# Multiply-adds with a factor of 1.0 read from a column in SBUF, and fewer pieces a map, in a deformable-convolution kernel

## The chip, the cores and the metric

The kernel runs on one core of a Trainium2 chip. The metric is the device time of one execution in microseconds; of several executions the median counts. Engines are called TensorE (PE in the rows; PEld is its weight load), VectorE (DVE), ScalarE (ACT), GpSimd (POOL) and SyncE (SP).

## The reference

Input x is 4 images of 128 channels and 80 x 80 pixels in float32. What is computed, cut to what matters:

```
out_normal = conv3x3(x, w_normal)
offset     = conv3x3(x, [w_offx, w_offy])            # 18 channels: dy, dx of 9 taps
out_x      = deform_conv(x, offset, w_dx)            # bilinear samples at 9 shifted taps
out_y      = deform_conv(x, offset, w_dy)
out        = conv3x3(concat(out_normal, out_x, out_y), w_fusion)     # 384 -> 128 channels
out        = relu(bn1(out))
out        = bn2(conv3x3(out, w_conv2))
return relu(out + x)
```

`deform_conv` takes, for each pixel and tap, the four corners around a shifted position, weighs them bilinearly and multiplies the sample by the tap's 128 x 128 weights.

## The kernel before, in words

The work is cut into 40 strips of 8 rows (640 pixels, 5 tiles of 128 pixels; 10 strips an image), and a loop of 44 steps (`run_steps`) is written out for each engine. Step i deals with the samples of strip i, and in the same step with later stages of earlier strips: the sums for the fusion convolution of strip i-1, that convolution for strip i-2, the last convolution for strip i-4. A step has nine parts, one for each tap k. `SLICES` says which pieces of the convolutions ("O" offsets, "F" fusion, "N" normal, "C" last) TensorE does within each tap. The order of each engine's instructions is the order of this code; between engines there are only semaphores.

**Samples.** GpSimd issues an indirect DMA for each tile and tap (L350, 45 a strip, 1800 in all): for 128 pixels it fetches the cell with the corners, by indices in SBUF that VectorE computed (`indices`, L717 to L743). `cells` has 15 slots (`GSLOTS`), and a gather waits until the slot's earlier user has been read (`mixed_done`, L348) and until TensorE is within 25 tiles (`pace`, L349). For the first image the table is x itself and ScalarE makes the upper product (L567); for the other images the table holds slopes, which VectorE makes from x (`slopes`, L892, two pieces in each of the first 27 steps). VectorE mixes the two rows of corners (L756: five multiply-adds of 256 elements a tap, whose factor is a column of `wgt` in SBUF), ScalarE makes the left product (L575, in the rows under the helper's L535), and VectorE adds the right one (L762: five of 128 elements). TensorE turns the sample (L431), ScalarE copies it out as a high part (`samp_hi`, L534), VectorE subtracts that for the low part (`samples_low`, L708), and TensorE multiplies high and low parts (`three`, L386: L388, L391, L394).

**High and low parts.** Each convolution runs in float32r as three products of high and low parts. The high part is a ScalarE copy (L534); the low part is VectorE's `low` (L706 to L708): source minus high part, a tensor-tensor subtraction.

**The fusion convolution.** It works on pairs of rows of three maps `raw` (the three concatenated inputs), on four kinds of rows held in `d_raw`/`d_hi`/`d_lo`, 16 rows of 82 each: rows 0 to 7 hold differences of rows two apart (`zs`, `last_row`), rows 8 to 11 sums, rows 12 to 15 differences of pairs (`sums`). VectorE makes them with `combine` (L830 to L832), a scalar-tensor-tensor instruction, a x 1.0 + b or - b, whose factor 1.0 is a constant within the instruction. In the rows `d_raw` is called `d_lo_f`.

VectorE's program in a step (L896 to L966), per tap k: `last_row` (k = 1), `sample` for tap k + 2, `samples_low` for k + 1, `indices` at k = 3, `last_row_low` at k = 2, a piece of `slopes` at k = 2 and 6, then what follows on a finished piece of a convolution:
- k = 4 (F, 1): L925, L927 (both read PSUM), `sums`: 6 combines of 320 elements
- k = 5 (F, 2): L934, `sums_low`: 6 subtractions of 320 elements
- k = 6 (F, 3): L941, `zs`: 6 combines of 240 elements and one for the first row; then L950, two multiply-adds of 320 elements with constant 0.0, which make the low part of the intermediate map `mid`
- k = 7 (N, 0): `zs_low`: 3 subtractions of 320 and 3 of 240 elements
- k = 8 (N, 1): `x_low`, one subtraction of 820 elements

ScalarE waits for `sums_done` and `zs_done` before its one copy for each (`sums_high` L610, `zs_high` L615), and before it overwrites `raw` (L678, L679). The first four steps use `FIRST_SLICES`.

Of the kernel before, what the change touches and what calls it, by code (L numbers as in the profile page):

```python
# [7 lines left out]
F32 = mybir.dt.float32  # L8
F32R = mybir.dt.float32r
I32 = mybir.dt.int32  # L10
ALU = mybir.AluOpType
# [3 lines left out]
B, C, H, W = 4, 128, 80, 80  # L15
TAPS = 9
EPS = 1e-5
ROWS = 8
# [83 lines left out]

BN_STEPS = 10
NIDX = 10
NCONST = 128 + 2 * TILES * TAPS + 4 * (STEPS + 1)


class Flags:
# [30 lines left out]
def at_least(eng, sem, value):  # L139

    if isinstance(value, int) and value <= 0:
        return
    eng.wait_ge(sem, value)


def deform_block(nc, x, xflat, xpair, weights, bn, const, out):
    ctx = ExitStack()
    with ctx:
# [24 lines left out]
        base_y = cst[:, 128:128 + PER].rearrange("p (j k) -> p j k", k=TAPS)  # L173
        base_x = cst[:, 128 + PER:128 + 2 * PER].rearrange("p (j k) -> p j k", k=TAPS)
        per_strip = 128 + 2 * PER

        x_raw = sb("x_raw", [128, SLOT])
        x_hi = sb("x_hi", [128, 2, SLOT_ROWS, PITCH], F32R)
# [352 lines left out]
        def _(eng):  # L531
# [82 lines left out]

            def zs_high(s):  # L615

                at_least(eng, zs_done, 7 * s + 7)
                copy(d_hi[:, :, 0:Z_ROWS - 1, 1:1 + W], d_raw[:, :, 0:Z_ROWS - 1, 1:1 + W]).then_inc(zs_hi, 1)
                at_least(eng, last_done, s)
                copy(keep[:], raw[:, :, ROWS - 2:ROWS, :]).then_inc(keep_done, 1)  # L620

            def step(i, par, fl):
                for k in range(TAPS):
# [21 lines left out]
                    for job, q in fl.done[k]:  # L645
# [30 lines left out]
                        if job == "N" and fl.strip:  # L676
                            rows = slice(q * HR, q * HR + HR)
                            at_least(eng, sums_done, 6 * i)  # L678
                            at_least(eng, zs_done, 7 * i)  # L679
                            at_least(eng, keep_done, i)  # L680
                            at_least(eng, n_done, 2 * i + q + 1)
                            copy(raw[:, 0, rows, :], work[q][:, 0:HALF].rearrange("p (r w) -> p r w", w=W))\
                                .then_inc(n_out, 1)
                            if q == 1 and fl.load:
                                x_high(i + 2, par)
# [19 lines left out]
        def _(eng):  # L705
# [123 lines left out]

            def combine(dst, a, b, op):  # L830

                return eng.scalar_tensor_tensor(out=dst, in0=a, scalar=1.0, in1=b, op0=ALU.mult, op1=op)  # L832

            def sums(s):

# [8 lines left out]
            def zs(s):  # L844

                for g in range(3):
                    to = d_raw[:, g, :, 1:1 + W]
                    combine(to[:, 1:HR, :], raw[:, g, 0:HR - 1, :], raw[:, g, 2:HR + 1, :], ALU.subtract).then_inc(zs_done, 1)
                    combine(to[:, HR:Z_ROWS - 1, :], raw[:, g, HR - 1:ROWS - 2, :], raw[:, g, HR + 1:ROWS, :],
                            ALU.subtract).then_inc(zs_done, 1)  # L850
                to = d_raw[:, :, :, 1:1 + W]
                if s % STRIPS:
                    at_least(eng, keep_done, s)
                    ins = combine(to[:, :, 0, :], keep[:, :, 1, :], raw[:, :, 1, :], ALU.subtract)
                else:
                    ins = eng.tensor_scalar(to[:, :, 0, :], raw[:, :, 1, :], -1.0, None, ALU.mult)
                ins.then_inc(zs_done, 1)

            def sums_low(s):

                at_least(eng, sums_hi, s + 1)
                for g in range(3):
                    for first in (SUM_ROW, DIFF_ROW):
                        rows = slice(first, first + PAIRS)
                        ins = low(d_lo[:, g, rows, 1:1 + W], d_raw[:, g, rows, 1:1 + W], d_hi[:, g, rows, 1:1 + W])
                ins.then_inc(sums_low_done, 1)

            def zs_low(s):

                at_least(eng, zs_hi, s + 1)  # L870
                for g in range(3):
                    for rows in (slice(0, HR), slice(HR, Z_ROWS - 1)):
                        ins = low(d_lo[:, g, rows, 1:1 + W], d_raw[:, g, rows, 1:1 + W], d_hi[:, g, rows, 1:1 + W])
                ins.then_inc(zs_low_done, 1)

            def last_row(s):
# [19 lines left out]
            def step(i, par, fl):  # L896
                for k in range(TAPS):
# [21 lines left out]
                    for job, q in fl.done[k]:  # L919
# [18 lines left out]
                        if job == "F" and q == T - 1:  # L938
# [5 lines left out]
                                zs(i - 1)  # L944
                            if fl.fuse:
                                at_least(eng, mid_hi_done, s + 1)
                                for half in range(2):
                                    rows = slice(half * HR, half * HR + HR)
                                    to = slice(1 + half * HR, 1 + half * HR + HR)
                                    ins = eng.scalar_tensor_tensor(  # L950
                                        out=mid[:, par, 1, to, 1:1 + W], in0=mid_f[:, rows, :], scalar=0.0,
                                        in1=mid[:, par, 0, to, 1:1 + W].bitcast(F32),
                                        op0=ALU.max, op1=ALU.subtract)
                                ins.then_inc(mid_lo_done, 1)
                        if job == "N" and q == 0 and fl.rows:
                            zs_low(i - 1)
# [14 lines left out]
def shape_constants():  # L971
# [8 lines left out]
    for s in range(STEPS + 1):  # L980
        b, r = s // STRIPS, s % STRIPS
        c[:, 128 + 2 * PER + 4 * s:128 + 2 * PER + 4 * s + 4] = (
            ROWS * r, max(b - 1, 0) * CELLS + LEAD * PITCH + 2, float(r != 0), float(r != STRIPS - 1))
    return c


# [40 lines left out]
```

## Time and profile before

| | us |
|---|---|
| median of 3 runs | 2667.61 |
| lowest, highest | 2664.85, 2673.97 |
| profiled execution | 2661.92 |
| its span | 2660.1 |

The profiled execution's mean granted TensorE clock is 0.966 of full speed. Busy shares of the span: TensorE 89% (15680 matmuls), VectorE 85% (5999 instructions), ScalarE 59%, GpSimd 75%. Busy time counts each engine's own instructions; semaphore waits and the issue of DMAs by SyncE are not in it. A share is an average over all stages, and an engine with a high share need not be the one that sets the time: for that one has to look at what ends each engine's idle time. Line numbers are those of the kernel before; a helper's line (L534, L535, L708, L832) stands for all who call it. Instructions of VectorE are recorded with overlap: the next one starts some 80 ns before the recorded end of the one ahead, so start-to-start times are shorter than the recorded durations.

### The profile page before, as it was taken

Reading aid. Unit: us, or ns where it says so; the run is one execution under the profiler, and the core shown is the slowest. Engines: PE = TensorE matmul, PEld = TensorE weight load, DVE = VectorE, ACT = ScalarE, POOL = GpSimd, SP = SyncE. Lnnn points to the kernel's source line nnn. Section 1 sums busy time; section 2 is a strip of 40 time slices with the busy share of each in tenths; the row PEclk is TensorE's granted clock in tenths of the full one; section 3 lists DMA queues with packets and bytes.
Section 4 is the critical chain, followed back from the end, with each engine's and each line's share of the span. In section 5 each row is a group of like instructions: output and inputs, shape, how many; then the busy total and the mean of one; then the engine's idle time right before and its main releaser. Section 6 shows DMA issues by size and latency. Waiting matters only on the chain.

```text
span 2660.1 us, 46973 instructions
## 1 busy us (share of the span) xinstructions
PE 2361.2 (89%) x15680; PEld 2323.2 (87%) x15680; DVE 2252.6 (85%) x5999; ACT 1565.6 (59%) x3577; POOL 2000.7 (75%) x1807
## 2 busy tenths in 40 slices
PE   3667899998999989989999999999989999899897
PEld 3567888998999989989899998998989988888897
DVE  5788888888998988988888898998888888888862
ACT  5777877877655555655555555555555555555531
POOL 7777777777777777777777777777777777777740
PEclk9879999999999999999999999999999999999999
DMA  7766777777777777777777777766666666666640
GB/s 223 214 213 211 241 229 222 227 226 222 220 226 241 220 227 232 228 233 233 233 231 240 239 238 225 234 206 206 200 205 195 207 197 204 198 196 206 194 126 25
DMA packets 179139, 564.89 MB, mean 212 GB/s; under 512 B 32721, under 2 KB 34129, under 8 KB 178769
## 3 DMA queue, kind: packets, MB, share of 16 engines
q0 software_dynamic: 144000, 471.97, 58.8%
q1 hardware_dynamic: 34896, 89.91, 9.6%
q8 instruction: 125, 2.05, 0.3%
q14 instruction: 118, 0.96, 0.1%
HBM read 527.41 MB, written 34.34 MB: 211 GB/s over the span
## 4 chain that ended last, share of the span: by engine, by line
DVE 38%; PE 26%; ACT 12%; DMA 11%; issue 9%; POOL 4%; ACTq 0%; DVEq 0%; POOLq 0%; SPq 0%
DVE mixed L756 9%; DMA cells<-slope_table,index 9%; DVE d_lo_f L832 6%; PE work L388 6%; PE work L391 5%; DVE d_lo L708 5%; PE work L394 5%; DVE samp L762 5%; DVE samp_lo L708 5%; ACT samp L535 4%; POOL cells L350 4%; ACT samp_hi L534 3%; DMA cells<-in_xpair,index 3%; PE turned L431 2%; PE acc L388 2%
## 5 line engine op out<-in xcount | busy, mean ns | idle before, releaser
L350 POOL DMA_INDIRECT cells<-slope_table,index x1350 | 1489.7, 1103 | 411.7 <-issue 208.8
L535 ACT ACTIVATE samp<-mixed,wgt 128x128 f32<-128x128 f32 x1800 | 649.1, 397 | 602.8 <-DVE mixed L756 600.0
L756 DVE SCALAR_TENSOR_TENSOR mixed<-cells,wgt 128x256 f32<-128x256 f32 x1350 | 575.6, 476 | 158.4 <-DMA cells<-slope_table,index 155.8
L350 POOL DMA_INDIRECT cells<-in_xpair,index x450 | 501.3, 1114 | 148.9 <-issue 86.3
L388 PE MATMUL work<-d_hi,w_hi 128*128 128x320 f32 x1440 | 480.9, 334 | 75.4 <-ACT off_s L534 73.6
L762 DVE SCALAR_TENSOR_TENSOR samp<-mixed,wgt,samp 128x128 f32<-128x128 f32 x1800 | 515.3, 345 | 29.8 <-ACT samp L535 29.3
L391 PE MATMUL work<-d_lo,w_hi 128*128 128x320 f32 x1440 | 464.4, 322 | 0.0
L394 PE MATMUL work<-d_hi,w_lo 128*128 128x320 f32 x1440 | 463.7, 322 | 0.0
L388 PE MATMUL acc<-samp_hi,w_hi 128*128 128x320 f32 x1440 | 451.3, 313 | 0.0
L391 PE MATMUL acc<-samp_lo,w_hi 128*128 128x320 f32 x1440 | 448.3, 311 | 0.0
L394 PE MATMUL acc<-samp_hi,w_lo 128*128 128x320 f32 x1440 | 447.3, 311 | 0.0
L431 PE MATMUL turned<-cst,samp 128*128 128x128 f32 x1800 | 264.5, 279 | 192.3 <-DVE samp_lo L708 173.9
L431 PEld LDWEIGHTS turned<-cst,samp 128*128 128x128 f32 x1800 | 213.6, 142 | 219.1 <-DVE samp L762 110.0
L388 PEld LDWEIGHTS work<-d_hi,w_hi 128*128 128x128 f32 x1440 | 282.3, 196 | 84.5 <-ACT off_s L534 82.2
L708 DVE TENSOR_TENSOR samp_lo<-turned,samp_hi 128x640 fp32r<-128x640 f32 x360 | 294.2, 817 | 47.7 <-ACT samp_hi L534 47.6
L391 PEld LDWEIGHTS work<-d_lo,w_hi 128*128 128x128 f32 x1440 | 283.7, 197 | 0.0
L394 PEld LDWEIGHTS work<-d_hi,w_lo 128*128 128x128 f32 x1440 | 283.2, 197 | 0.0
L534 ACT ACTIVATE d_hi<-d_lo_f 128x1920 fp32r<-128x1920 f32 (+2 forms) x120 | 153.2, 1277 | 213.0 <-DVE d_lo_f L832 207.2
L388 PEld LDWEIGHTS acc<-samp_hi,w_hi 128*128 128x128 f32 x1440 | 276.8, 192 | 0.0
L391 PEld LDWEIGHTS acc<-samp_lo,w_hi 128*128 128x128 f32 x1440 | 276.0, 192 | 0.0
L394 PEld LDWEIGHTS acc<-samp_hi,w_lo 128*128 128x128 f32 x1440 | 274.6, 191 | 0.0
L534 ACT ACTIVATE samp_hi<-turned 128x640 fp32r<-128x640 f32 x360 | 248.3, 690 | 20.5 <-PE turned L431 18.9
(86 smaller groups left out, 4198.5 us busy)
## 6 DMA issues: line engine op xcount, KB each, us to landing
cells<-slope_table,index POOLq DMA_INDIRECT x1350, 3.9
slope<-in_xpair SPq DMA_DIRECT2D x54, 384.0 KB, 5.3
slope_table<-slope SPq DMA_DIRECT2D x54, 384.0 KB, 4.1
x_raw<-in_xflat SPq DMA_DIRECT2D x40, 410.0 KB, 4.6
resid<-in_x SPq DMA_DIRECT2D x40, 320.0 KB, 5.2
out<-resid SPq DMA_DIRECT2D x40, 320.0 KB, 4.1
cells<-in_xpair,index POOLq DMA_INDIRECT x450, 3.9
w_lo_f<-in_weights SPq DMA_DIRECT2D x4, 576.0 KB, 8.6
```

Of the source, the lines that this page charges most:

```text
L350: eng.indirect_dma_start(out=cells[:, g, :], out_offset=None, in_=cell_rows, in_offset=bass.IndirectOffsetOnAxis(ap=index[:, par, j, k:k + ...
L388: ins = eng.matmul(dst, w_hi[:, w], hi, start=start, stop=False, skip_group_check=True)
L391: ins = eng.matmul(dst, w_hi[:, w], lo, start=False, stop=False, skip_group_check=True)
L394: return eng.matmul(dst, w_lo[:, w], hi, start=False, stop=stop, skip_group_check=True)
L431: ins = eng.transpose(turned[:, j * 128:(j + 1) * 128], samp[:, tp, j, :], ident)
L534: return eng.activation(dst, src, ACT.Copy)
L535: return eng.activation(dst, src, ACT.Copy, scale=scale)
L708: return eng.tensor_tensor(dst, src, hi.bitcast(F32), ALU.subtract)
L756: eng.scalar_tensor_tensor(out=both, in0=corner[:, g, :, 1, :], scalar=wgt[:, par, 1, 0, j, k:k + 1], in1=base, op0=ALU.mult, op1=ALU.add, ...
L762: eng.scalar_tensor_tensor(out=samp[:, tp, j], in0=mixed[:, tp, j, C:2 * C], scalar=wgt[:, par, 1, 1, j, k:k + 1], in1=samp[:, tp, j], op0 ...
L832: return eng.scalar_tensor_tensor(out=dst, in0=a, scalar=1.0, in1=b, op0=ALU.mult, op1=op)
```

## The change

The constant table gets two more columns, one of 0.0 and one of 1.0 (`zero`, `one`). `combine` takes its factor 1.0 from the column instead of from the instruction, for all its callers (sums, differences, last row, slopes). The low parts of the sums and of the differences are made by `combine` instead of the tensor-tensor subtraction, one instruction a map instead of two (640 and 560 elements). The differences are one instruction a map instead of two (480 elements), and the semaphore counts follow (4 a strip instead of 7). L950 becomes one instruction of 640 elements with its factor 0.0 from the column. The low parts of samples, x and weights, and `last_row_low`, stay as they are.

```diff
-NCONST = 128 + 2 * TILES * TAPS + 4 * (STEPS + 1)
+NCONST = 128 + 2 * TILES * TAPS + 4 * (STEPS + 1) + 2
...
+        zero, one = (cst[:, NCONST - n:NCONST - n + 1] for n in (2, 1))
...
-                at_least(eng, zs_done, 7 * s + 7)
+                at_least(eng, zs_done, 4 * s + 4)
...
-                            at_least(eng, zs_done, 7 * i)
+                            at_least(eng, zs_done, 4 * i)
...
-                return eng.scalar_tensor_tensor(out=dst, in0=a, scalar=1.0, in1=b, op0=ALU.mult, op1=op)
+                return eng.scalar_tensor_tensor(out=dst, in0=a, scalar=one, in1=b, op0=ALU.mult, op1=op)
...
-                    combine(to[:, 1:HR, :], raw[:, g, 0:HR - 1, :], raw[:, g, 2:HR + 1, :], ALU.subtract).then_inc(zs_done, 1)
-                    combine(to[:, HR:Z_ROWS - 1, :], raw[:, g, HR - 1:ROWS - 2, :], raw[:, g, HR + 1:ROWS, :],
-                            ALU.subtract).then_inc(zs_done, 1)
+                    combine(to[:, 1:Z_ROWS - 1, :], raw[:, g, 0:ROWS - 2, :], raw[:, g, 2:ROWS, :], ALU.subtract)\
+                        .then_inc(zs_done, 1)
...
-                    for first in (SUM_ROW, DIFF_ROW):
-                        rows = slice(first, first + PAIRS)
-                        ins = low(d_lo[:, g, rows, 1:1 + W], d_raw[:, g, rows, 1:1 + W], d_hi[:, g, rows, 1:1 + W])
+                    rows = slice(SUM_ROW, D_ROWS)
+                    ins = combine(d_lo[:, g, rows, 1:1 + W], d_raw[:, g, rows, 1:1 + W],
+                                  d_hi[:, g, rows, 1:1 + W].bitcast(F32), ALU.subtract)
...
-                    for rows in (slice(0, HR), slice(HR, Z_ROWS - 1)):
-                        ins = low(d_lo[:, g, rows, 1:1 + W], d_raw[:, g, rows, 1:1 + W], d_hi[:, g, rows, 1:1 + W])
+                    rows = slice(0, Z_ROWS - 1)
+                    ins = combine(d_lo[:, g, rows, 1:1 + W], d_raw[:, g, rows, 1:1 + W],
+                                  d_hi[:, g, rows, 1:1 + W].bitcast(F32), ALU.subtract)
...
-                                for half in range(2):
-                                    rows = slice(half * HR, half * HR + HR)
-                                    to = slice(1 + half * HR, 1 + half * HR + HR)
-                                    ins = eng.scalar_tensor_tensor(
-                                        out=mid[:, par, 1, to, 1:1 + W], in0=mid_f[:, rows, :], scalar=0.0,
-                                        in1=mid[:, par, 0, to, 1:1 + W].bitcast(F32),
-                                        op0=ALU.max, op1=ALU.subtract)
+                                ins = eng.scalar_tensor_tensor(
+                                    out=mid[:, par, 1, 1:1 + ROWS, 1:1 + W], in0=mid_f[:], scalar=zero,
+                                    in1=mid[:, par, 0, 1:1 + ROWS, 1:1 + W].bitcast(F32),
+                                    op0=ALU.max, op1=ALU.subtract)
...
+    c[:, NCONST - 1] = 1.0
```

## Rows read from the trace of the kernel before

**Rows 1.** The page: busy time by engine, and the chain of waits by engine.
```profile
PE 2361.2 (89%) x15680; PEld 2323.2 (87%) x15680; DVE 2252.6 (85%) x5999; ACT 1565.6 (59%) x3577; POOL 2000.7 (75%) x1807
...
DVE 38%; PE 26%; ACT 12%; DMA 11%; issue 9%; POOL 4%; ACTq 0%; DVEq 0%; POOLq 0%; SPq 0%
```

**Rows 2.** Groups of GpSimd (busy, mean ns, idle before), then durations min/median/max in ns.
```profile
L350 POOL DMA_INDIRECT cells<-slope_table,index x1350 | 1489.7, 1103 | 411.7 <-issue 208.8 <-DVE mixed L756 83.2 <-PE work L388 74.0
L350 POOL DMA_INDIRECT cells<-in_xpair,index x450 | 501.3, 1114 | 148.9 <-issue 86.3 <-DVE mixed L756 29.3 <-PE acc L388 12.4
...
L350 POOL DMA_INDIRECT cells<-slope_table,index x1350: 942/948/3922, 660.8 to 2560.6; - x193
L350 POOL DMA_INDIRECT cells<-in_xpair,index x450: 942/947/4781, 18.4 to 659.4; - x150
```

**Rows 3.** Timeline of GpSimd: start us, duration us, instruction, idle before and releaser.
```profile
18.44 3.27 POOL L350 DMA_INDIRECT cells<-in_xpair,index  x1 [8.24 <-DVE index L742]
...
1291.30 1.08 POOL L350 DMA_INDIRECT cells<-slope_table,index  x1 [0.31 <-issue]
...
1306.10 3.15 POOL L350 DMA_INDIRECT cells<-slope_table,index  x1 [0.30 <-issue]
1309.55 1.66 POOL L350 DMA_INDIRECT cells<-slope_table,index  x1 [0.30 <-PE work L388]
...
1350.36 3.29 POOL L350 DMA_INDIRECT cells<-slope_table,index  x1 [0.30 <-PE work L388]
...
1358.43 1.23 POOL L350 DMA_INDIRECT cells<-slope_table,index  x1 [0.30 <-issue]
...
2553.86 2.29 POOL L350 DMA_INDIRECT cells<-slope_table,index  x1 [0.30 <-issue]
...
2560.63 1.13 POOL L350 DMA_INDIRECT cells<-slope_table,index  x1 [0.30 <-issue]
```

**Rows 4.** Busy time by engine, from the last gather's end to the span's end.
```profile
2561.80:2660.10 98.30, 84.21 (x540) 83.23 (x538) 32.64 (x80) 22.22 (x40) 0.00 (x0) 0.97 0.08 28
```

**Rows 5.** Stretches of the transposes: strips 4 to 38, strip 17, strip 18 (second figure: length).
```profile
297.50:2512.30 2214.80, 226.31 (x1576) 183.72 (x1577) 257.33 (x315) 217.45 (x315) 0.98 0.71 220
...
1120.70:1187.30 66.60, 6.42 (x46) 5.28 (x46) 7.35 (x9) 6.22 (x9) 0.95 0.76 234
1187.30:1247.40 60.10, 6.41 (x45) 5.25 (x46) 7.35 (x9) 6.20 (x9) 1.00 0.72 224
```

**Rows 6.** VectorE's longest waits in strip 17, then in strip 18 (us, times, longest).
```profile
DVE mixed L756 <- DMA cells<-slope_table,index: 7.9, 8, 2.5
...
DVE samp_lo L708 <- ACT samp_hi L534: 1.6, 4, 0.8
```

**Rows 7.** Timeline of VectorE: start us, duration us of the group, instructions.
```profile
1290.28 2.49 DVE L832 SCALAR_TENSOR_TENSOR d_lo_f<-raw 128x320 f32<-128x320 f32 x6
...
1305.31 1.99 DVE L832 SCALAR_TENSOR_TENSOR d_lo_f<-raw 128x240 f32<-128x240 f32 x6
1307.21 0.40 DVE L832 SCALAR_TENSOR_TENSOR d_lo_f<-keep,raw 128x240 f32<-128x240 f32 x1
1307.53 0.88 DVE L950 SCALAR_TENSOR_TENSOR mid<-mid_f,mid 128x320 fp32r<-128x320 f32 x2
1308.34 2.06 DVE L756 SCALAR_TENSOR_TENSOR mixed<-cells,wgt 128x256 f32<-128x256 f32 x5
...
1350.34 2.49 DVE L832 SCALAR_TENSOR_TENSOR d_lo_f<-raw 128x320 f32<-128x320 f32 x6
1352.75 2.06 DVE L756 SCALAR_TENSOR_TENSOR mixed<-cells,wgt 128x256 f32<-128x256 f32 x5
...
1357.97 2.53 DVE L708 TENSOR_TENSOR d_lo<-d_lo_f,d_hi 128x320 fp32r<-128x320 f32 x6
1360.41 2.05 DVE L756 SCALAR_TENSOR_TENSOR mixed<-cells,wgt 128x256 f32<-128x256 f32 x5
```

**Rows 8.** VectorE's groups by shape: busy us, mean ns of one, idle before.
```profile
L727 DVE SCALAR_TENSOR_TENSOR pos<-off_s,cst 128x45 f32<-128x45 f32 x40 | 10.7, 268 | 1.4
...
L739 DVE SCALAR_TENSOR_TENSOR above<-cell_f 128x45 f32<-128x45 f32 x40 | 8.5, 212 | 0.0
```

## The prediction, before the kernel was changed

> **What bounds the kernel now.** I read the page first. TensorE is busy 89%, VectorE 85%, GpSimd 75%, and the chain of waits gives VectorE 38% and GpSimd only 4% [rows 1]. Read alone, that says "VectorE, then TensorE", and GpSimd looks free for a quarter of the time. The groups of GpSimd correct this. It issues 1800 gathers of mean 1.103 us (1.114 in the first image), with 411.7 + 148.9 us "idle" before them, mostly put down to "issue" [rows 2]. That idle time is no wait: in the timeline it is 0.30 us before every gather, whichever engine is named as releaser [rows 3]. So 1800 x 0.30 = 540 us of it is the gathers' own issuing, and little is left. Busy plus issuing is 1991 + 540 = 2531 us, and the time from the first gather (18.4) to the end of the last (2561.8) is 2543 us [rows 2, 3]. **GpSimd never stops**; it sets the time, with some 98 us behind its last gather in which the last strips are finished [rows 4].
>
> Are the others free? A strip (nine taps, 45 gathers) takes 2214.8 / 35 = 63.3 us over strips 4 to 38. But strip 18 took 60.1 us and strip 17 took 66.6 us [rows 5]. In strip 17 VectorE waited 7.9 us for gathered cells; in strip 18 its longest wait is 1.6 us in total, for ScalarE, and cells are not among its waits [rows 6]. So 60.1 us is what TensorE, VectorE and ScalarE need when the cells are there, and the rest is the gathers' pace.
>
> Why does a gather take 1.103 us, where the shortest is 942 ns and the median 948 [rows 2]? There are long ones: 76 of over 1.9 us (mean 3.01; the first, of 18.44, and the last, of 2553.86, stand in [rows 3]), and 55 of the gathers right behind them also take 1.72 us on average; the other 1669 take 1.00. I laid GpSimd's timeline over VectorE's [rows 3, 7]. The gather of 1306.10 (3.15 us) begins within L832's run of differences (from 1305.31), and ends 0.90 us behind the start of the first L756 (1308.34), that is, one undisturbed gather behind it. The gather of 1350.36 (3.29 us) begins as L832's sums begin (1350.34) and ends 0.90 us behind L756 at 1352.75. The same holds through L950, which follows the differences. So a gather that begins within a back-to-back run of multiply-adds with **constant** factor and both inputs in SBUF stands until the run is over. Of the 76 long ones 58 begin within L832. Not each run closes: the gather of 1291.30, within the sums from 1290.28, took only 1.08 us. Two other kinds do not hold it that way, though both their inputs lie in SBUF too: the subtractions L708 (the gather of 1358.43, within the run from 1357.97 to 1360.41, took 1.23 us, a wait of 0.28 to the end of the piece of 0.41), and L756, whose factor is a **column**, behind whose start the long ones end.
>
> **The change part by part.** VectorE first. Start to start, L832 of 320 elements takes 2.41 / 6 = 0.402 us and of 240 takes 1.90 / 6 = 0.317 [rows 7], so 1.05 ns an element and 0.066 us fixed. A factor from a column costs more: 45 elements take 268 ns with one (L727), 212 without (L739) [rows 8], so +0.056 us. A strip then gets:
> - sums: 6 x 0.402 = 2.41 becomes 6 x 0.458 = 2.75: +0.34
> - differences (480 elements, 3 for 6) and their first row: 2.22 becomes 3 x 0.626 + 0.37 = 2.25: +0.03
> - L950, 640 elements in one piece: 0.81 becomes 0.79: -0.02
> - low parts of the sums: 2.44 becomes 3 x 0.79 = 2.38: -0.06
> - low parts of the differences (560): 3 x 0.402 + 3 x 0.317 = 2.16 becomes 3 x 0.71 = 2.13: -0.03
> - last row +0.06; slopes +0.06 for each of 54.
>
> That is +0.26 us a strip in the taps where TensorE waits for VectorE, and 0.06 for the last row, which lies in a tap where VectorE waits for cells. If that cover goes, it costs 40 x 0.06 = 2 us. In total VectorE gets 40 x 0.32 + 3 = 16 us more. The constants' load grows by two columns: nothing, within a load already made. The waits on the count 4 s + 4 replace those on 7 s + 7; ScalarE waits for the whole set before and after, so nothing is late by it.
>
> GpSimd: what goes. A closed run costs, by the gather of 1306.10 and the one behind it, (3.15 - 0.95) + (1.66 - 0.95) = 2.91 us [rows 3]. 58 of them are 169 us. What comes: a gather within a column-factor piece waits for that piece's end. The bounds are nothing and a whole piece (0.46 to 0.79 us); I take a third of the piece, since the subtraction row shows 0.28 in a piece of 0.41 and most gathers (median 948) show none. About 4.6 gathers a strip begin in the sums, differences, last row and L950 (6 us of them, a gather each 1.3 us), at a third of a mean piece of 0.54, 0.18; 3.5 in the low parts at a third of 0.75, 0.25, of which 0.45 us is there today. Together 0.83 + 0.87 - 0.45 = 1.25 us a strip, 50 us. Net 169 - 50 = 119 us, 3.0 us a strip: GpSimd's own pace becomes 63.3 - 3.0 = 60.3 us.
>
> The rest of the kernel needs 60.1 + 0.26 + 0.06 (slopes) = 60.4. So **the gain is cut off by the next bound**, VectorE and TensorE in turn. Two bounds this close don't give the larger one exactly, since what one lacks in a strip is not made up in the next; I add 0.6 us (between 0 and the 3 us by which strips differ today): 61.0. Then 35 strips x (63.3 - 61.0) = 80 us. From the first four strips and the end I take nothing. The profiled execution took 2661.9 us (span 2660.1), so 2582; the median of the runs is 5.7 us above it, hence **2587 us**, 3% faster.
>
> One rule speaks against this. What the rows show is that the kind of factor decides how long a gather stands [rows 3, 7]. The Trainium skill ("SBUF — State Buffer", Who interferes with whom) says only that a VectorE instruction with two SBUF inputs contends with a GpSimd instruction that reads SBUF, and that the lock is held for the whole instruction. By that rule the kind of factor changes nothing and pieces of double length lock for longer; the time would be that of the first rival below, not 2587 us.
>
> **Rivals.**
> - *Locks go by instruction, not by run*. GpSimd could always slip in between two instructions and what matters is their length. Then the sums stay as they are, and longer pieces and VectorE's 0.32 us a strip come on top: 1.25 us of new waits a strip, without the 2.91s going: 35 x 1.25 = +44 on the median, **2712**. It decides if a column-factor run of sums, with its 0.46 us pieces, closes as before. Against it: gathers end behind the first L756, not behind one piece of L832. For it: L756 runs in fives, so a run of six or seven such instructions was never seen. Chance 0.07.
> - *VectorE sets the end as the chain says* (38%) and GpSimd's pace follows it: +16 us, **2684**. Against it: no gather waited over its 0.30. Chance 0.03.
> - *The gap opened by the column is sometimes missed* (some sums runs close today, some do not; L756 has stretched gathers too): half of the 2.91s remain, so GpSimd gains 85 - 50 = 35 us: **2633**. Chance 0.15.
> - *The first bound is further off*: strips 4 to 38 fall to 60.2 and the first four gain too: 35 x 3.1 = 109, **2559**. Chance 0.05.
> - *No change that can be seen*: relief and longer locks cancel. Chance 0.04.
>
> The forecast itself has the remaining 0.66.
>
> **Numbers.** The range reaches from 2553 (the waits of new pieces at their lower bound, the next bound at 60.2, and some us of the first strips) to 2640 (half the runs still close); 0.14 of the chance lies above it. A measurement of this kernel tells 0.3%, some 8 us, from no change: faster 0.86, same 0.04, slower 0.10.
>
> **What would show it.** Right: GpSimd's gathers of over 1.9 us nearly gone, and their mean 1.103 - 119 / 1800 = 1.04 us; VectorE (L756) waits less for cells; the spans of strips near 61 us and more even; L832 at 0.54 us for 320 elements (L832 as it is, plus 0.056), low parts of 640 elements in three pieces; ScalarE's offsets no longer hold up TensorE. Then GpSimd would show waits above 0.30 us, since it is no longer the one that never stops. Wrong: 3 us gathers within L832 as before (the first rival, or the third if half), or gathers that are short while the strips stay at 63 us, which would mean that 60.1 us is no floor that can be kept from strip to strip.

## The result, and the profile after

| | before | after |
|---|---|---|
| median, us | 2667.22 (4 runs) | 2797.19 (4 runs) |
| lowest, highest | 2664.85, 2673.97 | 2786.12, 2805.11 |
| profiled execution, its span | 2661.92, 2660.1 | 2786.12, 2784.3 |

The ratio is 1.048, with a 95% interval of 1.0439 to 1.0521: **slower by 130 us**, where 80 us less were forecast and 2640 was the end of the range. (Lines below are one higher than before: L350 is now L351, L756 is L757, L832 is L833; L950 is L948.)

The page of the changed kernel, beside [rows 1]:

```profile
PE 2395.6 (86%) x15680; PEld 2347.6 (84%) x15680; DVE 2271.9 (82%) x5599; ACT 1565.4 (56%) x3577; POOL 2124.3 (76%) x1807
...
PE 30%; DVE 26%; DMA 18%; issue 10%; ACT 10%; POOL 6%; ACTq 0%; POOLq 0%; DVEq 0%; SPq 0%
...
L757 DVE SCALAR_TENSOR_TENSOR mixed<-cells,wgt 128x256 f32<-128x256 f32 x1350 | 582.8, 479 | 252.9 <-DMA cells<-slope_table,index 249.2
```

VectorE has 19 us more work, but the span grew by 124. Of the chain, gathers and their transfers now hold 24% where they held 15%, and VectorE waits 249 us for cells. The engine to look at is again GpSimd. Its groups (as in [rows 2]), then its durations (min/median/max in ns):

```profile
L351 POOL DMA_INDIRECT cells<-slope_table,index x1350 | 1583.0, 1173 | 411.3 <-issue 254.7 <-DVE mixed L757 81.4 <-PE acc L389 45.4
L351 POOL DMA_INDIRECT cells<-in_xpair,index x450 | 531.6, 1181 | 148.3 <-issue 88.7 <-DVE mixed L757 28.6 <-PE acc L389 13.8
...
L351 POOL DMA_INDIRECT cells<-slope_table,index x1350: 942/949/5202, 690.3 to 2683.2; - x193
L351 POOL DMA_INDIRECT cells<-in_xpair,index x450: 942/947/5566, 17.6 to 689.1; - x150
```

The idle time is what it was, 0.31 us a gather, and the median gather too. What grew is the long ones. I call **standing time** what the gathers take beyond an undisturbed 0.946 us each: 1583.0 + 531.6 - 1800 x 0.946 = 412 us, where before it was 1991.0 - 1702.8 = 288 us. The difference, 124 us, is that of the spans. 118 gathers take over 1.9 us (76 before).

Busy time in stretches of the transposes: strips 4 to 38 (second figure: length), and all instructions from the last gather's end to the end of the span, beside [rows 4, 5]:

```profile
302.00:2636.60 2334.60, 232.61 (x1575) 185.19 (x1576) 257.71 (x315) 217.29 (x315) 0.96 0.69 209
...
2684.40:2784.30 99.90, 84.64 (x529) 83.44 (x527) 32.63 (x60) 22.21 (x40) 0.01 (x1) 0.92 0.08 28
```

A strip takes 2334.6 / 35 = 66.7 us instead of 63.3; the tail hardly changed (99.9 us for 98.3). So the loss lies in every strip, in the gathers. Their timeline (start us, duration us, idle before):

```profile
1161.66 1.21 POOL L351 DMA_INDIRECT cells<-slope_table,index  x1 [0.30 <-PE acc L389]
1163.17 1.29 POOL L351 DMA_INDIRECT cells<-slope_table,index  x1 [0.30 <-issue]
1164.76 2.99 POOL L351 DMA_INDIRECT cells<-slope_table,index  x1 [0.30 <-DVE mixed L757]
1168.05 0.96 POOL L351 DMA_INDIRECT cells<-slope_table,index  x1 [0.30 <-issue]
1169.32 5.20 POOL L351 DMA_INDIRECT cells<-slope_table,index  x1 [0.30 <-issue]
1174.82 0.94 POOL L351 DMA_INDIRECT cells<-slope_table,index  x1 [0.30 <-issue]
```

and VectorE's, in the same stretch (start, duration of the group):

```profile
1161.17 2.47 DVE L833 SCALAR_TENSOR_TENSOR d_lo<-d_lo_f,cst,d_hi 128x640 fp32r<-128x640 f32 x3
1163.55 2.06 DVE L757 SCALAR_TENSOR_TENSOR mixed<-cells,wgt 128x256 f32<-128x256 f32 x5
1165.53 1.40 DVE L763 SCALAR_TENSOR_TENSOR samp<-mixed,wgt,samp 128x128 f32<-128x128 f32 x5
1166.84 0.82 DVE L709 TENSOR_TENSOR samp_lo<-turned,samp_hi 128x640 fp32r<-128x640 f32 x1
...
1168.57 1.98 DVE L833 SCALAR_TENSOR_TENSOR d_lo_f<-raw,cst 128x480 f32<-128x480 f32 x3
1170.45 0.47 DVE L833 SCALAR_TENSOR_TENSOR d_lo_f<-keep,cst,raw 128x240 f32<-128x240 f32 x1
1170.83 0.89 DVE L948 SCALAR_TENSOR_TENSOR mid<-mid_f,cst,mid 128x640 fp32r<-128x640 f32 x1
1171.63 2.07 DVE L757 SCALAR_TENSOR_TENSOR mixed<-cells,wgt 128x256 f32<-128x256 f32 x5
1173.71 1.52 DVE L763 SCALAR_TENSOR_TENSOR samp<-mixed,wgt,samp 128x128 f32<-128x128 f32 x5
```

Take 0.95 us from the end of a gather: that is when it was let in. The gather of 1169.32 begins in the second of the differences, which now read their factor from a column as all behind them do, and is let in at 1173.57, as the last L757 ends and L763 starts 0.1 us late: the run was **not** opened by the column, and it no longer ends where L757 begins. The gather stood through eight boundaries. The gathers of 1161.66 and 1163.17 begin within low parts and are let in at 1161.92 and 1163.51, each as a piece ends. But then the next one, of 1164.76, begins 1.25 us on, just as the fourth L757 starts (1163.55 + 3 x 0.40), and stands until L709, which reads PSUM, at 1166.8.

Counted over the trace: of the long gathers before, 55 began in sums or differences and were let in at the first L756 behind them, with 2.20 us of standing each. In the changed kernel 29 that begin there stand until L763 starts, 3.74 us each; 74 begin in L757 and L763 (13 before).

### The profile page after: what moved, and what is told of

It reads as the page before. It is cut to its first block, busy times and chain, and to the rows that moved or that the text cites. A ratio compares the mean times of both kernels' runs of the same rounds, so it can differ in the third digit from the quotient of the medians.

```text
span 2784.3 us, 46573 instructions
## 1 busy us (share of the span) xinstructions
PE 2395.6 (86%) x15680; PEld 2347.6 (84%) x15680; DVE 2271.9 (82%) x5599; ACT 1565.4 (56%) x3577; POOL 2124.3 (76%) x1807
## 4 chain that ended last, share of the span: by engine, by line
PE 30%; DVE 26%; DMA 18%; issue 10%; ACT 10%; POOL 6%; ACTq 0%; POOLq 0%; DVEq 0%; SPq 0%
DMA cells<-slope_table,index 13%; PE work L389 7%; PE work L392 6%; PE work L395 6%; DVE mixed L757 6%; POOL cells L351 6%; DVE d_lo_f L833 5%; DMA cells<-in_xpair,index 4%; ACT samp L536 4%; DVE samp L763 4%; DVE samp_lo L709 4%; DVE d_lo L833 3%; PE turned L432 3%; ACT samp_hi L535 3%; PE acc L389 2%
## 5 line engine op out<-in xcount | busy, mean ns | idle before, releaser
L351 POOL DMA_INDIRECT cells<-slope_table,index x1350 | 1583.0, 1173 | 411.3 <-issue 254.7
L757 DVE SCALAR_TENSOR_TENSOR mixed<-cells,wgt 128x256 f32<-128x256 f32 x1350 | 582.8, 479 | 252.9 <-DMA cells<-slope_table,index 249.2
L351 POOL DMA_INDIRECT cells<-in_xpair,index x450 | 531.6, 1181 | 148.3 <-issue 88.7
L763 DVE SCALAR_TENSOR_TENSOR samp<-mixed,wgt,samp 128x128 f32<-128x128 f32 x1800 | 514.8, 347 | 33.1 <-ACT samp L536 32.5
L432 PE MATMUL turned<-cst,samp 128*128 128x128 f32 x1800 | 271.5, 284 | 268.9 <-DVE samp_lo L709 238.2
L709 DVE TENSOR_TENSOR samp_lo<-turned,samp_hi 128x640 fp32r<-128x640 f32 x360 | 294.6, 818 | 40.0 <-ACT samp_hi L535 39.8
```

What stands on the lines that cost most here:

```text
L351: eng.indirect_dma_start(out=cells[:, g, :], out_offset=None, in_=cell_rows, in_offset=bass.IndirectOffsetOnAxis(ap=index[:, par, j, k:k + ...
L432: ins = eng.transpose(turned[:, j * 128:(j + 1) * 128], samp[:, tp, j, :], ident)
L709: return eng.tensor_tensor(dst, src, hi.bitcast(F32), ALU.subtract)
L757: eng.scalar_tensor_tensor(out=both, in0=corner[:, g, :, 1, :], scalar=wgt[:, par, 1, 0, j, k:k + 1], in1=base, op0=ALU.mult, op1=ALU.add, ...
L763: eng.scalar_tensor_tensor(out=samp[:, tp, j], in0=mixed[:, tp, j, C:2 * C], scalar=wgt[:, par, 1, 1, j, k:k + 1], in1=samp[:, tp, j], op0 ...
```

## The experiments

Each was timed against the kernel before on the same chip. Its median there was 2664.64 us for e1 to e4, 2675.49 for e5 and e8 to e10, 2668.80 for e7 and e11 to e13, and 2674.43 for e14 and e15. So a difference of medians between two of these groups, or against the changed kernel, is good to some 10 us; the ratios are free of that. The whole of them first; standing time and the number of gathers over 1.9 us are from each profiled execution:

| kernel | median, us | ratio to before, 95% | standing, us | over 1.9 us |
|---|---|---|---|---|
| before | 2664.64 to 2675.49 | 1 | 288 | 76 |
| after | 2797.19 | 1.048 [1.0439, 1.0521] | 412 | 118 |
| e1 column in combine only | 2702.02 | 1.0127 [1.0093, 1.0162] | 336 | 91 |
| e2 joined pieces only | 2686.10 | 1.0081 [1.0055, 1.0106] | 327 | 88 |
| e3 sums as tensor-tensor | 2666.27 | 1.0001 [0.9982, 1.0020] | 284 | 77 |
| e5 one increment a set | 2674.92 | 0.9991 [0.9969, 1.0013] | 293 | 83 |
| e11 sums written as float32r | 2671.28 | 1.0016 [0.9991, 1.0040] | 302 | 85 |
| e12 other second input | 2665.55 | 0.9990 [0.9964, 1.0015] | 293 | 82 |
| e7 after, low parts subtracted | 2685.62 | 1.0073 [1.0046, 1.0100] | 329 | 89 |
| e8 after, constant in mid | 2771.00 | 1.0349 [1.0301, 1.0397] | 394 | 116 |
| e14 after, two memsets | 2724.81 | 1.0177 [1.0151, 1.0203] | 361 | 110 |
| e15 after, memset in samples | 2752.85 | 1.0289 [1.0247, 1.0331] | 380 | 76 |
| e9 after, twelve memsets | 2633.63 | 0.9843 [0.9807, 0.9880] | 251 | 41 |
| e4 before, thirteen memsets | 2565.79 | 0.9627 [0.9598, 0.9655] | 186 | 55 |
| e10 joined pieces, ten memsets | 2563.57 | 0.9576 [0.9542, 0.9610] | 187 | 38 |
| e13 the same, nine more in samples | 2528.27 | 0.9483 [0.9442, 0.9524] | 133 | 4 |

Span less standing time is 2366 to 2373 us in the first twelve rows (before 2660.1 - 288.2 = 2371.9, after 2372.5, e15 2370.0), 2378 to 2379 in e9, e4 and e10, and 2389 in e13. **While GpSimd never stops, the time is a constant plus what the gathers stand**; only the last four begin to meet another bound.

### The parts of the change, one at a time

**e1**, the column in `combine` alone:

```diff
-                return eng.scalar_tensor_tensor(out=dst, in0=a, scalar=1.0, in1=b, op0=ALU.mult, op1=op)
+                return eng.scalar_tensor_tensor(out=dst, in0=a, scalar=one, in1=b, op0=ALU.mult, op1=op)
...
```

> The kernel before with one edit: the factor 1.0 of sums, differences, last row and slopes comes from a column; pieces, low parts and L950 as before. Theory A (a gather that starts within a back-to-back run of two-SBUF-input instructions of one kind stands until the run is broken, by another kind of instruction, one that reads PSUM, or an idle moment): the sums and differences are now of the same kind as L756 and L762 behind them, closed runs reach into these, some gathers take about 5 us, and most of the 130 us are there: 2740 to 2800 us. Theory B (longer pieces lock longer, the factor only costs 0.056 us a piece): 2668 to 2690 us, long gathers as before. Theory of the prediction (the column opens the lock): under 2620 us.

It is slower by 1.3%: the part that was to bring the gain loses by itself. The time lies in none of the three ranges; gathers of some 5 us, as theory A had them, are there. GpSimd's timeline, and VectorE's:

```profile
1003.17 3.99 POOL L351 DMA_INDIRECT cells<-slope_table,index  x1 [0.30 <-issue]
```

```profile
1001.49 2.86 DVE L833 SCALAR_TENSOR_TENSOR d_lo_f<-raw,cst 128x320 f32<-128x320 f32 x6
1004.26 2.07 DVE L757 SCALAR_TENSOR_TENSOR mixed<-cells,wgt 128x256 f32<-128x256 f32 x5
1006.52 1.52 DVE L763 SCALAR_TENSOR_TENSOR samp<-mixed,wgt,samp 128x128 f32<-128x128 f32 x5 [0.19 <-ACT samp L536]
```

The gather begins in the fourth of six column-factor sums and is let in at 1006.21, as the fifth L757 ends and VectorE stands idle for 0.19 us. 19 long gathers end like this. 34 are still let in at the first L757; behind the differences L950 still has its constant, and there all 33 boundaries from it to L757 let the gather in. The opposite step, from the differences with their column to L950 with its constant, let in none of 36.

**e2**, the joined pieces alone, with constants and tensor-tensor low parts:

```diff
-                    for rows in (slice(0, HR), slice(HR, Z_ROWS - 1)):
+                    for rows in (slice(0, Z_ROWS - 1),):
...
```

> The kernel before with the pieces joined as in the change (differences 480, low parts 640 and 560, L950 640 elements), but constants within the instruction and low parts still tensor-tensor subtractions. Theory A: closed runs end at L756 as before, 2650 to 2690 us, no gather over 4 us but the first. Theory B: most of the 130 us, 2740 us or more.

0.8% slower, in theory A's range. The two parts together are 21 + 37 = 58 us of the 130; the rest needs the low parts.

**e7**, the changed kernel with subtractions in the low parts, still one piece a map:

```diff
-                    ins = combine(d_lo[:, g, rows, 1:1 + W], d_raw[:, g, rows, 1:1 + W],
-                                  d_hi[:, g, rows, 1:1 + W].bitcast(F32), ALU.subtract)
+                    ins = low(d_lo[:, g, rows, 1:1 + W], d_raw[:, g, rows, 1:1 + W], d_hi[:, g, rows, 1:1 + W])
...
```

> The changed kernel with the low parts as tensor-tensor subtractions again, in one piece a map. Both kinds let a gather in at the end of a piece in all traces so far, and differ by 0.056 us a piece. If that is all: 6 x 0.06 us a strip less for VectorE and hardly anything for the gathers, 2775 to 2800 us. If the column in the low parts counts beyond that (by the run of one kind that it makes with L756 behind it): 2740 to 2770 us.

Both expectations missed: it gives back some 110 of the 130 us. GpSimd's groups:

```profile
L351 POOL DMA_INDIRECT cells<-slope_table,index x1350 | 1517.7, 1124 | 411.3 <-issue 250.4 <-DVE mixed L757 65.5 <-PE acc L389 55.8
L351 POOL DMA_INDIRECT cells<-in_xpair,index x450 | 514.3, 1143 | 148.2 <-issue 90.2 <-DVE mixed L757 24.7 <-PE acc L389 15.8
```

Where the standing time lies, by the instruction in which the gather begins (us; sums over each trace):

| begins in | before | after | e1 | e7 | e14 | e15 | e13 |
|---|---|---|---|---|---|---|---|
| sums, differences, mid | 130 | 155 | 157 | 157 | 92 | 187 | 17 |
| their low parts | 13 | 35 | 15 | 25 | 43 | 36 | 29 |
| x_lo | 7 | 16 | 2 | 14 | 19 | 15 | 13 |
| L757 | 102 | 145 | 124 | 91 | 162 | 115 | 50 |
| L763 | 27 | 48 | 25 | 31 | 34 | 15 | 13 |
| others | 10 | 13 | 12 | 11 | 12 | 13 | 11 |

The low parts' factor costs 10 us in the low parts themselves. 71 us of it lie in L757 and L763, which the edit doesn't touch, and there in one place: in the ten instructions that follow low parts. Gathers that begin in those stand 25 us in the kernel before, 28 in e7 and 105 in the changed kernel; those that begin in any other L757 or L763 stand 103, 94 and 88. The same place in e7, GpSimd, then VectorE:

```profile
745.14 1.17 POOL L351 DMA_INDIRECT cells<-slope_table,index  x1 [0.30 <-issue]
746.61 0.95 POOL L351 DMA_INDIRECT cells<-slope_table,index  x1 [0.30 <-DVE mixed L757]
```

```profile
743.20 2.28 DVE L709 TENSOR_TENSOR d_lo<-d_lo_f,d_hi 128x640 fp32r<-128x640 f32 x3
745.40 2.06 DVE L757 SCALAR_TENSOR_TENSOR mixed<-cells,wgt 128x256 f32<-128x256 f32 x5
```

The first gather is let in as the last low part ends, and the next begins just as the fourth L757 starts (745.40 + 3 x 0.40), like the one of 1164.76 in the changed kernel. But it stands not at all, where that one stood 2.04 us. In e7 37 gathers come back in this way to the fourth L757 behind low parts, and 1 stands beyond it; in the changed kernel 42, and 25 stand beyond it. Both sets begin 17 ns behind the start in the median. (The profiled execution of e7 took 2704 us, 19 more than its median, so that the columns differ by 83 us and not by 110.)

**e8**, the changed kernel with the constant back in L948:

```diff
-                                    out=mid[:, par, 1, 1:1 + ROWS, 1:1 + W], in0=mid_f[:], scalar=zero,
+                                    out=mid[:, par, 1, 1:1 + ROWS, 1:1 + W], in0=mid_f[:], scalar=0.0,
```

> The changed kernel with one edit: the piece that makes the low part of mid (L950 of before) has its factor 0.0 as a constant again. In the runs so far a closed run always opened where L756, with a column, followed a piece with a constant, and mostly not where it followed a piece with a column. If so, gathers of over 4 us behind the differences go, and the time falls from 2797 by 40 to 80 us, to 2720 to 2755. If the length of the pieces is what counts: 2790 to 2800.

26 us less than the changed kernel (35 by the ratios): the direction of the first account, but short of its 40 to 80. GpSimd, then VectorE:

```profile
1104.92 3.15 POOL L351 DMA_INDIRECT cells<-slope_table,index  x1 [0.30 <-issue]
```

```profile
1106.44 0.82 DVE L948 SCALAR_TENSOR_TENSOR mid<-mid_f,mid 128x640 fp32r<-128x640 f32 x1
1107.17 2.07 DVE L757 SCALAR_TENSOR_TENSOR mixed<-cells,wgt 128x256 f32<-128x256 f32 x5
```

Let in at 1107.12, the first L757, as before. All 34 gathers that reached this boundary were let in; in the changed kernel, where the piece ahead of it has a column too, 10 of 32.

### What it is in the sums that closes

Three kernels change one property of the sums and differences of the kernel before; a fourth, the increments.

**e3**, tensor-tensor instead of multiply-add:

```diff
-                return eng.scalar_tensor_tensor(out=dst, in0=a, scalar=1.0, in1=b, op0=ALU.mult, op1=op)
+                return eng.tensor_tensor(dst, a, b, op)
```

> The kernel before with sums, differences, last row and slopes as plain tensor-tensor additions and subtractions, pieces as before. The run of the low parts (tensor-tensor too) hardly ever held a gather before. If that is due to the kind: the gathers of over 1.9 us go and the time falls by 60 to 100 us, to 2570 to 2610. Theory A without anything about the kind itself: runs close as before and end at L756, 2650 to 2685 us.

**e5**, the semaphore's increment on the last piece of a set only:

```diff
-                    combine(to[:, DIFF_ROW:D_ROWS, :], odd, even, ALU.subtract).then_inc(sums_done, 1)
+                    ins = combine(to[:, DIFF_ROW:D_ROWS, :], odd, even, ALU.subtract)
+                ins.then_inc(sums_done, 1)
...
```

> The kernel before, but of the sums only the last piece increments its semaphore, and of the differences only the last too (as the low parts do); nothing else. Theory C (a piece that increments a semaphore keeps the next gather out; the low parts hold none because only their last piece increments): the long gathers within L832 go and the time falls by 60 to 100 us. Theory A (the run itself, whatever it increments): 2655 to 2680 us, some 76 long gathers as before.

**e11**, the results as float32r, in the low parts' own tile (so rounded, which leaves nearly nothing for the low parts):

```diff
-                    to = d_raw[:, g, :, 1:1 + W]
+                    to = d_lo[:, g, :, 1:1 + W]
...
```

> The kernel before, but sums and differences are written as float32r, as the low parts are, so that they are rounded and their low parts are next to nothing; instructions and times otherwise the same. If the output's type is what lets a gather in between two low parts and not between two sums: the long gathers within L832 go, 2570 to 2610 us. If not: 2655 to 2680 us.

**e12**, a block of the constant table as second input (so the fusion convolution's inputs have other values):

```diff
-                    combine(to[:, SUM_ROW:SUM_ROW + PAIRS, :], even, odd, ALU.add).then_inc(sums_done, 1)
+                    combine(to[:, SUM_ROW:SUM_ROW + PAIRS, :], even, other, ALU.add).then_inc(sums_done, 1)
...
```

> The kernel before, but the second input of sums and differences is a block of the constant table instead of the other row of the same map, so that the two inputs come from different tensors, as with the low parts; the values of the fusion convolution are then others, the work is the same. If two inputs out of one tensor keep the gather out: the long gathers within L832 go, 2570 to 2610 us. If not: 2655 to 2680 us.

All four take the time of the kernel before, and 77 to 85 gathers are long. Neither the factor's kind (e1), nor the instruction, nor output type, increments or the shared input tensor is by itself what makes a run of sums close. The reason why gathers within low parts are let in at a piece's end is therefore none of these alone.

### Opening the runs

**e4**, the kernel before with a memset of one element of a spare tile (`gap`) ahead of each piece of the sums and differences, 13 a strip:

```diff
+                    gap()
                     combine(to[:, SUM_ROW:SUM_ROW + PAIRS, :], even, odd, ALU.add).then_inc(sums_done, 1)
+                    gap()
                     combine(to[:, DIFF_ROW:D_ROWS, :], odd, even, ALU.subtract).then_inc(sums_done, 1)
...
```

> The kernel before with a one-element memset of a spare column ahead of each piece of the sums and differences (13 a strip, perhaps 0.07 us each, 0.9 us of VectorE a strip). Theory A: each memset breaks the run, gathers of over 1.9 us nearly go, GpSimd gains some 3 to 4 us a strip, of which 0.9 is lost again where VectorE bounds: 2590 to 2640 us. Theory B, and any in which the lock is not opened by another kind of instruction: 2668 to 2710 us.

3.7% **faster** than before, with 520 more instructions; the gain is larger than expected (2590 us was the lower end). No long gather begins in the sums and differences any more. Strip 17 (second figure: its length), and what L757 still waits:

```profile
1090.20:1150.40 60.20, 6.43 (x46) 5.30 (x46) 7.39 (x9) 6.20 (x9) 1.00 0.77 241
```

```profile
L757 DVE SCALAR_TENSOR_TENSOR mixed<-cells,wgt 128x256 f32<-128x256 f32 x1350 | 561.2, 478 | 29.8 <-DMA cells<-slope_table,index 28.2
```

Strip 17 took 66.6 us before; now it takes 60.2, where strip 18 had shown 60.1 [rows 5].

**e9**, the changed kernel with 12 such memsets, between the pieces and behind the sums and L948:

```diff
...
                                 ins.then_inc(mid_lo_done, 1)
+                                gap()
```

> The changed kernel with a one-element memset ahead of each piece of the sums and differences, one behind the sums and one behind the low part of mid (12 a strip, 0.07 us each). If the extra 130 us are all closed runs: gathers of over 1.9 us nearly go and the time is that of the next bound, 2565 to 2590 us. If part of it is longer pieces or VectorE's own time: 2620 us or more.

**e10**, the joined pieces of e2 with memsets between them:

```diff
+                    gap()
                     combine(to[:, 1:Z_ROWS - 1, :], raw[:, g, 0:ROWS - 2, :], raw[:, g, 2:ROWS, :], ALU.subtract)\
                         .then_inc(zs_done, 1)
...
```

> The joined pieces with constants and tensor-tensor low parts (as in e2), plus the memsets ahead of the sums' and differences' pieces. Against e4 it saves VectorE 3 + 3 + 3 + 1 pieces' fixed times of 0.066 us and 3 memsets a strip, 0.8 us. If VectorE bounds the strips of e4 at 60.2 us: 59.4 us and 2540 to 2560 us. If the gathers bound it: 2560 to 2575 us, since longer pieces hold a gather a little longer.

e9 lies in the range of its second account, e10 in the one in which the gathers bound it. With the memsets the column costs 70 us still (e9 against e10): gathers stand longer to a piece's end, and those that begin in L757 and L763 stand 145 us for 114. Joining the pieces, which cost 21 us without them, costs nothing (e10 against e4).

**e14** has only the two memsets where L757 follows the sums and L948, and leaves all boundaries within the runs as they are:

```diff
                     combine(to[:, DIFF_ROW:D_ROWS, :], odd, even, ALU.subtract).then_inc(sums_done, 1)
+                gap()
...
```

> The kernel after, with a one-element memset at two places of a strip only: behind the sums and behind the low part of mid, where the first L757 follows. If what the column cost in the sums and differences is the boundary to L757 (opened 55 times in the kernel before, no longer opened in the changed one, where 29 gathers stand from the differences through five L757), the gathers that stand from there into L763 are gone, each 2 us shorter: 2715 to 2765. If the boundary is nothing by itself and the loss is where the gathers come to lie, it stays at 2780 to 2800.

In the range of the first account, 72 us less than the changed kernel. GpSimd, then VectorE (this kernel's lines are higher: L833 is L842, L757 is L766):

```profile
1214.38 3.22 POOL L352 DMA_INDIRECT cells<-slope_table,index  x1 [0.31 <-issue]
```

```profile
1213.63 1.97 DVE L842 SCALAR_TENSOR_TENSOR d_lo_f<-raw,cst 128x480 f32<-128x480 f32 x3
...
1216.70 0.48 DVE L766 SCALAR_TENSOR_TENSOR mixed<-cells,wgt 128x256 f32<-128x256 f32 x1
1216.72 0.06 DVE L753 MEMSET spare<- 128x1 f32 x1
```

The gather that began in the second of the differences is let in at 1216.65, at the memset, as [rows 3, 7] had it at L756. 36 gathers end there, at 2.04 us of standing; none reaches L763 from the sums. Behind the low parts nothing was opened, and there the standing stays, 113 us for 105.

**e15**, a memset between L757 and L763 of each tap of the changed kernel, and none in the sums:

```diff
                     ).then_inc(mixed_done, 1)
+                gap()
                 for j in range(TILES):
...
```

> The kernel after, with a one-element memset between L757 and L763 of every tap, and nothing in the sums, differences and low parts. 74 gathers of over 1.9 us begin in L757 and L763 of the changed kernel and stand 119 us beyond an undisturbed one. If the low parts' loss is that gathers let in at their ends come back at an L757 start and stand through the samples, most of it is open again: 2675 to 2715. If the loss is in the runs of sums and differences themselves, at most 10 us: 2785 to 2800.

Missed: 44 us less, where 82 to 122 were expected. The long gathers of L757 and L763 did shorten, from 119 to 34 us. But more gathers then fell into the runs of sums, 49 long ones for 37, and these rose from 132 to 171 us. What is opened in one run is partly paid in the next.

**e13**, e10 with the memset of e15 added:

> As e10, plus a one-element memset ahead of each group of L762 (one a tap). In e10 strips without a wait for cells took 59.5 us and most took 61.1, and gathers that begin with a group of L762 often stand until its end. If the memset opens that: gathers gain 0.5 to 1 us a strip, VectorE loses 0.6, both bounds meet near 60.2, 2540 to 2560 us. If VectorE's loss weighs more: 2565 to 2580 us.

The fastest kernel of the study: **2528.27 us, 5.2% less than before** (0.9442 to 0.9524), and below both ranges expected. Nothing reads what the memsets write. Its durations of gathers, and twenty strips (of 59.6 us):

```profile
L351 POOL DMA_INDIRECT cells<-slope_table,index x1350: 940/948/1676, 633.3 to 2419.3; - x193
```

```profile
657.60:1849.10 1191.50, 128.44 (x901) 105.57 (x901) 147.22 (x180) 124.13 (x180) 1.00 0.78 239
```

From the second image on no gather takes over 1.68 us.

## Why the prediction was wrong

**What bounds the kernel: right.** GpSimd hardly stops (13 of its gathers waited over 0.35 us, 4 us more than their issue in all, so "no gather waited over its 0.30" is not quite so), and the span follows the gathers' standing time to a few us in twelve kernels. The next bound of 60.1 us a strip was about right: strip 17 takes 60.2 us in e4, and strips 4 to 38 take 60.9 on average there, beside the 61.0 that was taken. It is no floor for other instructions, since e13 takes 59.6.

**The price of the column: right.** Start to start a sum of 320 elements takes (1004.26 - 1001.49) / 6 = 0.462 us in e1, forecast 0.458. VectorE's busy time rose by 19 us for 16.

**The new waits to a piece's end: about right in the low parts**, 22 us more for 17.

**The step that failed** is "a gather that begins within a back-to-back run of multiply-adds with **constant** factor and both inputs in SBUF stands until the run is over", with its other half, that L756, "whose factor is a **column**", does not hold it that way. From this came "58 of them are 169 us" of relief. The rows showed one boundary, from a constant's piece to a column's, at which gathers were let in. I took the column for what opens; it was the **step from the one to the other** (let in 61 of 61 times in the kernel before, and 34 of 34 at mid in e8). With a column on both sides this boundary lets a gather in 10 of 32 times behind mid, and the run goes on through five L757 into L763. The step the other way lets none in (0 of 36 in e1). So of the 169 us nothing went (sums, differences and mid rose from 130 to 155 us, at fewer but longer ones), and each closed run that passes on costs 1.5 us more. e1 shows it for the column alone. e8 shows it at the boundary itself, by the constant put back behind the differences; e14 opens it there and behind the sums with a memset each, and takes 72 us back. The trace of before held the warning, and the third rival named it: of 201 boundaries between two L756 that a waiting gather met, 57 kept it out, and ten gathers already stood over 0.95 us from within L756, a run of columns, nine of them until L708 (17.7 us in all). I gave 0.66 to what two timelines seemed to show.

**The first rival had half of it.** Its deciding point, a column-factor run that closes as before, came true; but its mechanism, a lock for one instruction, did not, and its price of 1.25 us a strip (2712) was too low. The Trainium skill ("SBUF — State Buffer", SBUF: two separate sides) has such a lock last for the whole instruction. The trace disagrees: the gather of 1169.32 stood 4.25 us, through eight boundaries between instructions of at most 0.9 us.

**What no case had** is the larger half, some 110 us by e7. The cost of a wait was taken where it occurs. But each gather begins 1.25 us after the one ahead was let in, and L757 starts each 0.40 us: a gather let in as the last low part ends comes back at the start of the fourth L757. Over the traces of all kernels but e14 and e15 some 2900 gathers begin within 0.04 us behind a start of L757, and 640 of them stood beyond that instruction; those that begin later in it nearly always wait for its end only. Of the gathers beginning in L757, 50 stood over 0.95 us (10 before).

This phase is needed, but it is not what the column changed: in e7, with subtractions in the low parts, nearly as many gathers come back to the same instant of the fourth L757, and 1 of 37 is shut out, where in the changed kernel 25 of 42 are. What the low parts' column does is that the instructions **behind** them shut gathers out. That place holds 77 us (105 for 28) of the 83 by which the two profiled executions differ. e15 agrees: a memset between L757 and L763 takes 85 us of long standing away.

**Open.** Why gathers within low parts are nearly always let in at a piece's end (114 of 118 in both kinds), while those in sums are not, and what decides for a gather at a start whether it is shut out. The kind of the two neighbours does not settle it alone: from the last low part with its column to L757 with its own, 47 of 47 were let in. Nor does the kind of instruction ahead: in e3 the sums are tensor-tensor as the low parts of e7 are, and all 22 gathers that came back to the fourth L757 behind them were shut out. e3, e5, e11 and e12 rule out four reasons and give none.

## What to carry to other kernels

Where GpSimd issues indirect DMAs without a pause, sum up their standing time first; then look for long back-to-back runs of VectorE instructions with two inputs in SBUF, across the borders of loops and helpers, and put an instruction between them that doesn't read SBUF twice: a memset of one element, or one that reads PSUM, if there is one to move. A boundary that lets gathers in was worth more here than a shorter instruction, and an edit that makes two neighbours alike can close it. Price such an edit by a run, since what one run lets go the next may catch.

## What the runs showed of the hardware

- A gather can stand through a run of back-to-back VectorE instructions: 4.25 us beyond its 0.95 over eight boundaries in the changed kernel, and at most 5.56 us over 13 in e7 (the gather of 226.79). What always let a waiting gather in: an idle moment of VectorE (131 of 131 within and behind L756 in the kernel before), an instruction that reads PSUM (55 of 55 from L762 to L708 there), a memset (502 of 502 over six kernels).
- The Trainium skill ("SBUF — State Buffer", Who interferes with whom) says that a VectorE instruction with at most one SBUF input, outside its two-port modes, does not contend with GpSimd. The trace agrees: the 187 gathers of the changed kernel that begin in `samp_lo`, which reads PSUM, stand 0.0 us together.
- A memset of one element is recorded at 59 ns. 760 of them, with the pieces joined, made the kernel 140 us faster.
- The Trainium skill ("VectorE: DVE Perf Modes", The TRN2 errata) advises tiles of at least 512 elements, so that a fixed cost per instruction is paid less often. The fixed cost is there [rows 7], but e2, which follows the advice in its low parts and L950 (560 and 640 elements), is 0.8% slower, and e4 with more and shorter instructions 3.7% faster: VectorE's time did not bound this kernel, its grip on GpSimd did.
